# A causal mask moved from a matmul of its own into 32 spare rows of the score operands

## The reference, cut to what matters

```
x = x + tanh(g_xattn) * attention(layernorm(x), ctx, ctx)     # 16 heads of 16, causal mask, softmax
x = x + tanh(g_ffn)   * moe(layernorm(x))                     # 8 experts, the 2 best, softmax of those
# attention: scores = q @ k.T / 4; scores = where(j <= i, scores, -inf); softmax; @ v; @ w_o.T + b_o
```

## Time and profile before

| | us |
|---|---|
| median of 3 runs (lowest, highest) | 983.84 (979.72, 990.62) |
| the profiled execution | 979.53 |
| its span, first to last instruction | 977.8 |
| busy: TensorE, VectorE, ScalarE, GpSimd | 887.0, 605.2, 444.2, 252.7 |
| first score product of group 0, of group 1 | 30.4, 53.6 |
| last score product of group 15 | 464.8 |
| first matmul of the experts | 512.0 |

### The profile page before, as it was taken

The page is one execution under the profiler, slowest core; times in us unless marked ns, Lnnn a source line. Parts: engine busy times, 40 slices in busy tenths (PEclk is TensorE's granted clock), DMA queues, the critical chain, the costliest instruction groups (busy, mean ns, idle before and its releaser), DMA issues. The chain is left out here.

```text
span 977.8 us, 25308 instructions
## 1 busy us (share of the span) xinstructions
PE 887.0 (91%) x7728; PEld 774.3 (79%) x7729; DVE 605.2 (62%) x1521; ACT 444.2 (45%) x962; POOL 252.7 (26%) x229
## 2 busy tenths in 40 slices
PE   4799999999999999999609999999899989999991
PEld 3688888888888888887508898899798979999880
DVE  3468788888688877777645565556456555556550
ACT  2354555555445545554205454455354444454440
POOL 2001233322033232223210223233313222232322
PEclk9799999999799979999658999999999999999996
DMA  7766877767587874767688632333222332332212
GB/s 161 135 128 173 192 192 190 167 177 167 164 190 195 195 187 101 169 178 231 220 314 321 168 61 47 52 57 52 47 45 46 51 54 38 49 54 41 29 23 24
DMA packets 86071, 124.34 MB, mean 127 GB/s; under 512 B 8928, under 2 KB 77664, under 8 KB 81760
## 3 DMA queue, kind: packets, MB, share of 16 engines
q1 hardware_dynamic: 70592, 102.90, 40.6%
q0 software_dynamic: 14304, 19.15, 12.3%
q10 hardware_dynamic: 1088, 1.11, 0.4%
HBM read 55.21 MB, written 42.75 MB: 100 GB/s over the span
## 5 line engine op out<-in xcount | busy, mean ns | idle before, releaser
L1289 PE MATMUL bank<-xh,wts 128*128 128x256 f16 x1872 | 216.6, 277 | 0.0
L1165 POOL DMA_INDIRECT out_rows<-yg,xs x78 | 126.9, 1627 | 346.8 <-ACT yg L1207 202.8
L1305 PE MATMUL bank<-wts,hh 128*128 x1872 | 210.6, 273 | 0.0
L1289 PEld LDWEIGHTS bank<-xh,wts 128*128 x1872 | 186.0, 99 | 23.9 <-issue 0.2
L1305 PEld LDWEIGHTS bank<-wts,hh 128*128 128x128 f16 x1872 | 183.2, 98 | 21.2
L1197 ACT ACTIVATE hf<-bank,b1t,gscale 128x256 f32<-128x256 f32 x312 | 154.8, 561 | 23.9 <-PE bank L1289 22.0
L906 PE MATMUL bank<-va,probs 128*128 128x17 f32 x1024 | 134.8, 265 | 7.6 <-DVE ao L626 7.6
L906 PEld LDWEIGHTS bank<-va,probs 128*128 128x128 f32 x1024 | 128.4, 197 | 10.1 <-DVE ao L626 7.4
L514 ACT ACTIVATE probs<-bank 128x512 f32<-128x512 f32 x128 | 76.5, 598 | 121.4 <-PE bank L891 120.7
L1207 ACT ACTIVATE yg<-yb,xs 128x256 f32<-128x256 f32 x78 | 35.4, 500 | 204.2 <-DVE yb L1246 198.9
L1236 DVE SCALAR_TENSOR_TENSOR hh<-hf,hscale,hh 128x512 f16<-128x512 f32 x156 | 117.2, 751 | 5.6
(11 more groups left out here) (168 smaller groups left out, 1201.9 us busy)
## 6 DMA issues: line engine op xcount, KB each, us to landing
wts<-in_W SPq DMA_DIRECT2D x16, 1024.0 KB, 7.9
split_weights<-wts SPq DMA_DIRECT2D x16, 1024.0 KB, 5.0
wts<-split_weights SPq DMA_DIRECT2D x16, 1024.0 KB
wts<-keys SPq DMA_DIRECT2D x96, 128.0 KB
wts<-queries SPq DMA_DIRECT2D x96, 128.0 KB
xs<-token_rows SPq DMA_DIRECT2D x39, 272.0 KB
xin<-in_x SPq DMA_DIRECT2D x16, 256.0 KB, 4.9
cin<-in_ctx_in SPq DMA_DIRECT2D x16, 256.0 KB, 5.2
```

The lines of the kernel that those rows point to most:

```text
L1165: pool.indirect_dma_start(out=out[:, :], out_offset=bass.IndirectOffsetOnAxis(ap=numbers, axis=0), in_=yg[m % 2][:, half, :], in_offset=No ...
L1289: last = pe.matmul(HB[c // 2][:, c % 2 * TILE:(c % 2 + 1) * TILE], wts[:, bass.ds(expert[1], 1), at:at + P], xh[b][:, xp, k, :], start=q = ...
L1305: last = pe.matmul(YB[b][:, half * D:(half + 1) * D], hh[b][:, hp, c, half * P:(half + 1) * P], wts[:, bass.ds(expert[0], 1), at:at + D], ...
```

## The change

The mask product is taken out. The 32 unused partitions of the stacked queries and keys are filled once, at the start, with constant rows. `qsteps` and `ksteps` are made on GpSimd by ten selections (five for `qsteps`, five for `ksteps`); SyncE then copies their partitions 96 to 127 into both buffers of queries and of keys, repeated over 16 heads and 2 sequences: four DMAs of 256 KB, each in pieces of 128 bf16 values. In the product of the two operands over 128 partitions these rows add nothing where the key is not later than the query and a very large negative number where it is. The four score products of a quad then run over 128 partitions, and each opens and closes its own accumulation. The transposed scores keep their mask product (L885).

The core of the diff:

```diff
+SPAN = 4
+STEP = 2.0 ** 31
+FUTURE = 2.0 ** 28
...
+        qfull = [stacked[:, 0, i] for i in range(2)]
+        kfull = [stacked[:, 1, i] for i in range(2)]
...
                         sp.wait_ge(consts, 2)
 
+                        sp.wait_ge(steps_made, 1)
+                        for i in range(2):
+                            for full, steps in ((qfull[i], qsteps), (kfull[i], ksteps)):
+                                sp.dma_start(full[STACK:P, :, :].rearrange("p h (b t) -> p (h b) t", b=GT),
+                                             steps[STACK:P, :].unsqueeze(1).to_broadcast([P - STACK, HEADS * GT, P])
+                                             ).then_inc(steps_placed, 16)
                         load(out[T:T + P, :], padrow[:, 0:D])
...
-                step.later(pool.memset(mask[:, :], 0.0))
+                step.later(pool.memset(qsteps[:, :], STEP))
+                step.later(pool.memset(ksteps[:, :], -FUTURE / STEP))
...
-                pool.affine_select(out=mask[:, :], in_=mask[:, :], compare_op=ALU.is_ge,
...
+                for i in range(SPAN + 1):
+                    step(pool.affine_select(out=qsteps[:, :], in_=qsteps[:, :], compare_op=ALU.is_ge,
...
+                for i in range(1, SPAN + 1):
+                    step(pool.affine_select(out=ksteps[:, :], in_=ksteps[:, :], compare_op=ALU.is_ge,
...
+                pool.affine_select(out=ksteps[:, :], in_=ksteps[:, :], compare_op=ALU.is_ge,
...
-                dve.wait_ge(consts, 10)
+                dve.wait_ge(consts, 9)
...
+                            if isinstance(g, int) and g == 0 and n == 0:
+                                pe.wait_ge(steps_placed, 16 * 4)
...
-                            pe.matmul(ps[:, :], ident16[:, :], mask[:, :].unsqueeze(1).to_broadcast([P, 4, P]),
-                                      start=True, stop=False)
                             for i, j in enumerate(pairs):
-                                last = pe.matmul(ps[:, i * P:(i + 1) * P], qst[par][:, 2 * j + odd, tok],
-                                                 kst[par][:, 2 * j + odd, tok], start=False, stop=i == 3)
+                                last = pe.matmul(ps[:, i * P:(i + 1) * P], qfull[par][:, 2 * j + odd, tok],
+                                                 kfull[par][:, 2 * j + odd, tok], start=True, stop=True)
```

More of the change, by code:

```diff
@@ L118, in bass_flamingo @@
         ident16 = sb("ident16", [P, P], BF16)
-        mask, maskT = sb("mask", [P, P], BF16), sb("maskT", [P, P], BF16)
+        qsteps, ksteps, maskT = (sb(name, [P, P], BF16) for name in ("qsteps", "ksteps", "maskT"))
         earlier = sb("earlier", [P, P], BF16)
@@ L165, in attention_and_routing @@
     (x, ctx_in, g_xattn, g_ffn, w_q, b_q, w_k, b_k, w_v, b_v, w_o, b_o, W1, b1, W2, Wr, br, out,
-     xs_dram, w_dram, bank, qst, kst, ident, negident, ident16, mask, maskT, earlier, ones16, rank1,
+     xs_dram, w_dram, bank, qst, kst, qfull, kfull, ident, negident, ident16, qsteps, ksteps, maskT, earlier, ones16, rank1,
      rank0, ones8, region0, base, mostsel, tgx, tgf, gates_in, power, wscale, wsquares, padrow,
@@ L169, in attention_and_routing @@
          "x", "ctx_in", "g_xattn", "g_ffn", "w_q", "b_q", "w_k", "b_k", "w_v", "b_v", "w_o", "b_o",
-         "W1", "b1", "W2", "Wr", "br", "out", "xs_dram", "w_dram", "bank", "qst", "kst", "ident",
-         "negident", "ident16", "mask", "maskT", "earlier", "ones16", "rank1", "rank0", "ones8", "region0",
+         "W1", "b1", "W2", "Wr", "br", "out", "xs_dram", "w_dram", "bank", "qst", "kst", "qfull", "kfull", "ident",
+         "negident", "ident16", "qsteps", "ksteps", "maskT", "earlier", "ones16", "rank1", "rank0", "ones8", "region0",
          "base", "mostsel", "tgx", "tgf", "gates_in", "power", "wscale", "wsquares", "padrow",
@@ L258, in attention_and_routing @@
         mask_ready = sem("mask_ready")
+        steps_made, steps_placed = sem("steps_made"), sem("steps_placed")
         dve_consts, waits_taken = sem("dve_consts"), sem("waits_taken")
@@ L424, in _ @@
                                    fill=1.0, base=0, pattern=[[-1, P]], channel_multiplier=1).then_inc(consts, 1)
-                pool.affine_select(out=mask[:, :], in_=mask[:, :], compare_op=ALU.is_ge,
-                                   fill=MASKED, base=0, pattern=[[-1, P]],
-                                   channel_multiplier=1).then_inc(consts, 1)
                 pool.affine_select(out=maskT[:, :], in_=maskT[:, :], compare_op=ALU.is_ge,
@@ L444, in _ @@
                           ).then_inc(numbers_made, 1)
+                for i in range(SPAN + 1):
+                    step(pool.affine_select(out=qsteps[:, :], in_=qsteps[:, :], compare_op=ALU.is_ge,
+                                            fill=STEP ** -i if i < SPAN else 0.0, base=i - 1 - SPAN * STACK, pattern=[[-1, P]],
+                                            channel_multiplier=SPAN))
+                for i in range(1, SPAN + 1):
+                    step(pool.affine_select(out=ksteps[:, :], in_=ksteps[:, :], compare_op=ALU.is_ge,
+                                            fill=-FUTURE * STEP ** (i - 1) if i < SPAN else 0.0, base=i - 1 - SPAN * STACK,
+                                            pattern=[[-1, P]], channel_multiplier=SPAN))
+                pool.affine_select(out=ksteps[:, :], in_=ksteps[:, :], compare_op=ALU.is_ge,
+                                   fill=0.0, base=SPAN * STACK, pattern=[[1, P]], channel_multiplier=-SPAN
+                                   ).then_inc(steps_made, 1)
                 def it(g, par, half):
```

## The result

The change takes 1025.34 us (median of 4 runs, 1021.66 to 1028.77) against 982.52 us for the kernel before (median of 4 beside it): a ratio of 1.042, 95% interval 1.034 to 1.050. It is slower. The 1012 us of the prediction were 13 too few; the time is inside the predicted range. The profiled execution took 1021.96 us (span 1020.1), 42.4 more than the one of before.

The account below looks back on a forecast made before the run. TensorE was taken to set the groups' pace, VectorE not far behind. Mask product -13, clock +43.9 and start +1.5 sum to +32.4 on the profiled 979.5 us: 1012 us, range 966 to 1042.

Parts of the forecast that it names:

- Mask product, step by step: Attention groups: dropping the 0.22 us product gains 0.88 us in each of 14 middle groups, -13 us with the last.
- steps 0, 2, 3 and 4: Half-head steps of a group where TensorE is back to back: gain 4 x 0.22 = 0.88 us.
- step 1: Step where the wk product waits for `cT`: the mask product's 0.22 us goes into this wait, gain nothing.
- steps 5 to 7: Steps between output projection and L906, set by VectorE's chain: 0.66 us of products turns into waiting, gain nothing.
- The wait ahead of the maxima's products and `ao`: TensorE ahead of L906 and L885: some 1.3 us of waiting together, where it was 0.67.
- The 128 partitions: Score products over 128 partitions instead of 96 cost the same: zero.
- The clock: Before the turn to a new group: falls in 13 of 14 at 4.4 us, less 13.3 already paid, +43.9 us.
- a sign against itself: Attention groups: forecast wrong if clock stays 1.00 in over half, or a fall lasts as short as 1.5 us.
- the margin was small beside 0.66 us: Stretch before the turn: losing 0.66 us of the densest work was judged enough for falls in 13 of 14.
- The start: Selections and four 256 KB DMAs ahead of the first keys: +1.5 us, bounds 0 and 32 us.
- The last group: Last attention group, shorter than the middle ones: counted with them in the mask product's -13 us.
- That the clock holds: Rival, stretch before the turn: no more falls than now and the gain stays, 968 or 953 us; chance 0.20.

Follow-up runs that it names:

- e4: The change plus five overwritten 512-column products per group at the turn (three ahead of maxima waits, two ahead of `ao`): 962.48 us, ratio 0.981.
- e7: The kernel before, mask product kept, plus three overwritten products per group at the turn (one in step 7, two ahead of `ao`): 970.66 us, ratio 0.987.
- e1: The change with one overwritten 512-column product put back ahead of the scores in every half-head step: 982.59 us, ratio 1.003.
- e2: The kernel before with the mask product taken out and nothing in its place, no constant rows or transfers: 1024.19 us, ratio 1.043.
- e3: The kernel before plus building the constant rows, the four transfers and their waits, with no product reading the rows: 984.43 us, ratio 1.0034.
- e8: e4 with the four transfers moved behind group 0's keys and added products in the last group: 959.75 us, ratio 0.975.
- e9: e8 with the transfers split: first buffer's two ahead of the keys, second buffer's two behind the queries: 962.97 us, ratio 0.979.
- e6: The change with only two overwritten products per group, ahead of the wait for `ao` at the turn: 970.37 us, ratio 0.988.
- e5: The change with five overwritten products per group, one in each of steps 1 to 5, none at the turn: 1017.02 us, ratio 1.035.
- e11: e9 with three instead of two added products ahead of `ao` at each turn: 953.89 us, ratio 0.969.
- e10: e9 with the transposed scores' mask product ahead of the maxima wait, added products in steps 6 and 7 cut from three to one: 972.09 us, ratio 0.992.

## Why the prediction was right in sign and too low

*Mask product, step by step: right.* The clean group is 0.89 us shorter, sized 0.88. By steps, steps 0, 2, 3 and 4 lost 0.22 us each (3.28 to 3.06, 4.00 to 3.78 twice, 2.92 to 2.70), step 1 nothing, and steps 5 to 7 together nothing (1.97, 2.22 and 4.15 became 1.75, 2.35 and 4.24). The wait ahead of the maxima's products and `ao` was to be 1.3 us, and is 0.34 + 0.53 + 0.45, taken as the prediction took it. e4 against e7 gives the 12.3 us again.

*The 128 partitions: right.* Zero in e1.

*The clock: right in mechanism and count, price somewhat high.* Thirteen of fourteen was the forecast and the trace. The earlier trace rows shows one of the two falls that the prediction reads there; the other stretch is this:

```profile
357.95:363.00 5.05, 5.05 (x26) 3.95 (x26) 3.39 (x15) 0.08 (x1) 0.54 (x1) 0.50 1.02 337
```

The falls cost 417.1 - 14 x 26.19 = 50 us, 3.9 each where 4.4 was taken: three groups had short spells that cost 1.5 to 2.2 (one as short as the 1.5 that the prediction named as a sign against itself), the other ten some 4.5 each. What was paid before comes to 392.8 - 14 x 27.07 = 13.8. Net 36.6, predicted 43.9. The judgement that the margin was small beside 0.66 us was the term that no row could give; e2 and e1 bear it out. That the count came out to the very group is luck: nine of the ten long falls follow on one another, in groups of 30.69 to 30.83 us, and whether one fall brings on the next was not tested.

*The start: mis-sized.* +3.2 us against +1.5 (e3: +3.5 in total), and outside the 2 us that the prediction allowed the first score. The prediction let the transfers use idle time of the queues and come ahead of the second group's loads and the keys alone. But SyncE's issues follow each other in one queue, and the four took it 5.9 us to issue, a time that the sum does not have: the padding row's loads, for which ScalarE waits ahead of the keys' second part, moved from 8.67 to 14.40 us as well. e8 shows that this wait is not the whole of it, and e9 that none of the cost is needed.

*The last group: missed.* The prediction gave it -0.7 us with the others. It has no projections of a next group and takes 28.9 us at 0.50 where it took 18.0 at 1.00, and the stretch to the experts follows at the half clock, +3.8. These 14.6 us are more than the whole error of 10. e6 shows it by itself: middle groups at 1.00, last group at 0.52; in e8 twelve more products there than in e4 bring it from 0.77 to 0.91. The missing mask products are not all of it, though: with them kept, or a product in their place, the last group took 22.0, 23.8 and 23.5 us in e1, e3 and e7, each with a fall in it, so the 18.0 of the one trace before are the best of four.

*The total.* It lies as near as it does by luck too: the falls cost 7.3 us less than the sum has, and the first group 1.8 less, against 1.7 more for the start, 15 for the last group and the stretch behind it, and 2 for the experts.

*The rivals.* That the clock holds had 0.20. TensorE's waits in the change, from the second middle group to the last of them (in total, times, longest):

```profile
PE bank L932 <- DVE ao L652: 5.9, 13, 0.5
PE bank L911 <- issue: 4.4, 12, 0.4
PE bank L911 <- DVE rowmax L702: 2.6, 13, 0.5
PE bank L835 <- ACT cT L545: 0.7, 2, 0.4
```

None is longer than 0.5 us, and twelve of the thirteen groups of this stretch fell. The Trainium skill, in "TensorE: Matmul & The Clock Gate", section "Why this matters for your kernels", asks that there be no long idle gaps between bursts of matmuls; that was kept here and was not enough. The copy on VectorE between series of matmuls that the same page of the Trainium skill, under "Loop structure matters more than you think", calls harmless is not this case: there the next matmuls follow immediately, here TensorE waits for VectorE's `ao`. That one wait, once in a group, left open or filled with two products, was the difference between thirteen falls and none (the change and e6); whether it is the idle time or the dense work in it that counts, no run here tells apart.

## What to carry to other kernels

Before taking dense work off TensorE, look for the thinnest stretch of the loop and ask what the granted clock does there; if falls occur already, the work that goes may be what holds the clock, and its place counts more than its length. Where waiting can't be avoided, a product whose result is overwritten is free in the wait (e4); the same products in busy steps did not hold the clock (e5). Judge an edit with the clock held on both sides too (e4 against e7): the change itself was worth 6 to 8 us, and the falls that it brought cost 37 us net in the middle groups alone.

## What was not expected of the hardware

- Two products of 0.22 us ahead of one wait of 0.45 us, which starts show as 0.61, took the thirteen falls of the clock away in the profiled execution (e6). The falls that other runs still showed go with what is left of that wait from start to start: none left with three products (e11, no falls), 0.16 or 0.17 us with two (e4 and e6 none, e8 two, e9 three; the traces of e4 and e6 are of their shortest executions, those of e8 and e9 of their longest), 0.38 in e10 (nine), 0.61 in the change (thirteen). It can't be that wait alone: the kernel before has 0.61 too, with its mask product beside it, and four. And e10 also moved a real product away from there; the two were not tried apart, so what is decisive in e10 stays open.
- Falls in the change's middle groups lasted 3.4 or 10.2 us. In its last group, which has no next group's projections, the clock stayed at 0.50 for the 28.9 us and on to the experts (0.50 over the next 51 us).
- The four transfers of constant rows kept SyncE issuing for 5.9 us (8.44 to 14.36), 0.7 us for each of the first two and 2.7 and 1.7 for the others, where a load from the parameters took 0.43.
